# Attention scores issued for two units at a time in the first stage of a transformer layer kernel

## The reference

```python
qkv = (x @ w_qkv).reshape(Bx, Lx, 3, NUM_HEADS, HEAD_DIM)
scores = jnp.einsum('bhqd,bhkd->bhqk', q, k) / np.sqrt(HEAD_DIM)
scores = jnp.where(causal, jnp.finfo(scores.dtype).min, scores)
out = jnp.einsum('bhqk,bhkd->bhqd', softmax(scores), v)
x = layernorm(x + out @ w_out)
# ternary: weights to -1, 0, 1 by |w| > 0.5 * mean|w|; the input over its rms
h = gelu(ternary_linear(x, w_up), approximate=False)
x = layernorm(x + ternary_linear(h, w_down))
```

## Time and profile before

| | us |
|---|---|
| median of 3 runs | 2260.82 (2260.28 to 2261.11) |
| the profiled execution | 2259.11 |
| its span, slowest core | 2257.2 (cores 2249.8 to 2257.2) |
| PE busy | 2135.0 (95%) |
| ACT busy | 1349.5 (60%) |
| DVE busy | 1237.7 (55%) |
| POOL busy | 355.3 (16%) |

### The profile page before, as it was taken

One profiled execution on the slowest core, in us unless ns is written; L12 is line 12 of the kernel. 1 busy time (PEld: TensorE's weight loads), 2 busy tenths in 40 slices (PEclk: granted clock), 3 DMA queues, 4 the chain that ended last, 5 costly groups with the idle time before them and its releaser, 6 DMA issues.

```text
span 2257.2 us, 54506 instructions; the slowest of 8 cores (2249.8 to 2257.2 us)
## 1 busy us (share of the span) xinstructions
PE 2135.0 (95%) x21250; PEld 1313.1 (58%) x21250; DVE 1237.7 (55%) x2100; ACT 1349.5 (60%) x1436; POOL 355.3 (16%) x574
## 2 busy tenths in 40 slices
PE   5999999998899999889999999999999999999998
PEld 2555555555455555466566656656656656566665
DVE  2455555677777533365566555645635545445654
ACT  1589888888788898732444444455465565755111
POOL 3222121222222122101100110110110110101110
PEclk9999999999999999989999999999999999999999
DMA  9135343353545113311000101100101100101100
GB/s 155 34 118 155 114 131 128 111 169 122 155 146 162 42 23 106 125 53 45 32 29 36 50 20 36 41 27 32 39 20 30 47 20 20 47 5 39 38 20 19
DMA packets 77946, 154.70 MB, mean 69 GB/s; under 512 B 27392, under 2 KB 45952, under 8 KB 76672
## 3 DMA queue, kind: packets, MB, share of 16 engines
q1 hardware_dynamic: 70880, 134.44, 17.8%
q0 software_dynamic: 6816, 16.78, 4.7%
HBM read 134.42 MB, written 33.55 MB: 74 GB/s over the span
## 4 chain that ended last, share of the span: by engine, by line
PE 84%; DVE 6%; ACT 5%; issue 4%; DMA 1%; DVEq 0%; POOL 0%; SPq 0%; ACTq 0%; POOLq 0%
PE mm L76 60%; PE sc L76 13%; PE pv L76 11%; ACT pb L76 3%; ACT L76 1%; DVE kt L76 1%; DVE wneg L76 1%; DMA xT<-xt 1%; DVE nrm L76 1%; DVE ast L76 1%; DMA yb<-x 1%; DVE vs L76 0%; DVE qt L76 0%; DVE pb L76 0%; DVE yb L76 0%
## 5 line engine op out<-in xcount | busy, mean ns | idle before, releaser
L76 ACT ACTIVATE pb<-sc,bias 128x1024 bf16<-128x1024 f32 (+3 forms) x1152 | 1160.7, 1042 | 449.8 <-PE sc L76 434.6
L76 PE MATMUL mm<-wdn,hT 128*128 128x512 fp8e4 x2048 | 479.3, 380 | 0.0
L76 PEld LDWEIGHTS pv<-vs,pb 128*128 128x128 bf16 x8448 | 365.5, 98 | 174.6 <-issue 48.0
L76 PE MATMUL pv<-vs,pb 128*128 128x65 bf16 x8448 | 410.1, 194 | 29.0 <-DVE ast L76 16.7
L76 ACT ACTIVATE hT<-mm 128x512 bf16<-128x512 f32 x256 | 152.9, 597 | 343.3 <-PE mm L76 342.7
L76 PEld LDWEIGHTS mm<-wdn,hT 128*128 128x128 bf16 x2048 | 186.6, 98 | 243.7 <-issue 51.7
L76 PE MATMUL mm<-xT,wq 128*128 128x512 bf16 x1024 | 307.9, 391 | 15.5 <-DMA xT<-xt 15.5
L76 PE MATMUL sc<-qt,kt 64*128 64x512 bf16 (+3 forms) x1440 | 270.0, 372 | 3.0 <-ACT pb L76 2.6
L76 PE MATMUL mm<-xnT,wupa 128*128 128x256 bf16 x2048 | 231.5, 274 | 2.3 <-ACT hT L76 1.3
L76 PEld LDWEIGHTS mm<-xnT,wupa 128*128 128x128 fp8e4 x2048 | 198.2, 98 | 28.7 <-issue 4.3
L76 DVE TENSOR_TENSOR hsq<-hT 128x512 f32<-128x512 bf16 x240 | 166.0, 692 | 56.2 <-ACT hT L76 52.1
(11 more groups left out here) (63 smaller groups left out, 1765.6 us busy)
## 6 DMA issues: line engine op xcount, KB each, us to landing
wr<-w_up SPq DMA_DIRECT2D x64, 512.0 KB, 3.6
wr<-w_down SPq DMA_DIRECT2D x64, 512.0 KB, 3.6
yb<-x SPq DMA_DIRECT2D x32, 512.0 KB, 3.2
out<-yb SPq DMA_DIRECT2D x32, 512.0 KB, 2.6
xT<-xt POOLq DMA_DIRECT2D x16, 512.0 KB, 35.9
wq<-w_qkv POOLq DMA_DIRECT2D x24, 256.0 KB, 8.9
att_s<-ast SPq DMA_DIRECT2D x40, 128.0 KB, 2.8
atto<-att_s SPq DMA_DIRECT2D x8, 640.0 KB, 4.2
```

What stands on the lines that cost most here:

```text
L76: ins = ops[op](*args, **kw)
```

## The change

The loop of the first stage takes the units two by two. It issues the scores of both, adds up their widths, works out the rate once, and then pulls, lets the weights go on and drains once for both, with the summed width. In the order on PE that gives: scores of u, scores of u + 1, the pieces of both, pv of u - 2, pv of u - 1.

```diff
-            for unit in units:
-                wide = min(4, 4 - (unit[2] - 4 * unit[1])) / 4.0
-                emit_qk(*unit)
-                left = work.left()
-                rate = left / max(to_do, 1.0)
+            for two_units in zip(units[0::2], units[1::2]):
+                wide = 0.0
+                for unit in two_units:
+                    wide += min(4, 4 - (unit[2] - 4 * unit[1])) / 4.0
+                    emit_qk(*unit)
+                rate = work.left() / max(to_do, 1.0)
                 if p == 0 and c < 5:
                     rate = max(rate, 2 * QKV_NS / (4 * c + 2.5))
                 to_do -= wide
                 work.pull(rate * wide)
                 if p > 0 or c >= 4:
                     side_pull(0.27 * wide)
                 drain(LAG)
```

## The result

| | before | after |
|---|---|---|
| median of 6 runs, us | 2260.97 (2259.44 to 2268.51) | 2309.39 (2305.59 to 2309.9, and one of 2432.63) |
| ratio, 95% interval | | 1.0206 (1.019 to 1.0223) |
| a later set of runs, ratio | | 1.0214 (1.0196 to 1.0232) |

The change makes the kernel 48 us slower; 2314 us were forecast, within 2280 to 2340.

The account below looks back on a forecast made before the run. PE was taken as the bound, ACT close behind. 16 - 6 + 45 + 5 - 4 = +56 us, less 3 for hidden DVE waits, gave 2312 us on the profiled execution, 2314 as median; range 2280 to 2340.

Parts of the forecast that it names:

- The bank stalls: First-stage norm and bound matmuls sharing a pair with their group's end wait 0.66 us for eviction: +45 and +5 us.
- The windows that keep a boundary: Norm and bound matmuls with pv and scores still between get 0.47 us more cover: -4 us.
- the walk over eight pairs: Pair spacings reckoned from PE work and exponential delay, scores 314.63 to 333.31 us: 18.68 becomes 19.06, with stalls 21.04.
- The hand-over: A pair's second scores wait for the previous pair's second exponential, 2.64 us spacing: net +16 us from the sixth chunk.
- the saving: First stage: a pair costs PE 0.21 us less than two units, at most 77 us over 366 pairs.
- ACT needs the same: four exponentials back to back take 4.43 us, 1.11 each: First stage: ACT needs 1.11 us per exponential, as PE needs 1.10 to 1.11 us per unit with one piece.
- +2 us at most, taken as nothing: Between chunks, 0.1 us less cover for DVE's output scaling, some 16 waits; assumed covered by PE's wait at second scores.
- What stays: Pieces, pv matmuls and DVE, POOL and SP instructions keep number and order; no new wait for pb.
- The signs: Profile after: score waits 40 us or more, blk and o64 some 75, spacings 2.2 and 2.64, stage some 975 us.
- The clock: Rival: the granted clock falls often in the first stage, adding some 25 us, 2340 us; chance 0.09.
- The drain rival: From scores to full-height matmuls, -0.21 us a pair wins if second scores seldom wait for ACT: 2230 us; chance 0.07.
- The upper bound: Half of the bank stalls double through DVE's queue, +22 us on top: 2338 us.

Follow-up runs that it names:

- after_again: The changed kernel run once more with no edit, for a profile to read: median 2308.3 us.
- half exponentials: First-stage exponentials over the left half of each head's columns only: changed kernel 2233.45 us, kernel before 2246.51 us.

## Why the prediction was right, and where it was not

**The bank stalls** were right in mechanism, and nearly in size. Along the trace of after_again, from the sixth chunk on, 75 norm and bound matmuls have their group's end in the same pair (74 counted ahead), with 65.1 us of stalls, a median of 0.68 us each and 1.32 us from the last matmul's start; the other 84 wait 7.4 us in all, where 8 were left by the estimate. (A stall is counted here with its 0.16 us of drain.) Over the whole stage the change brought 77 such matmuls into one pair with their group's end, 76 by the prediction. By idle time they waited 11.8 us in 19 places in the kernel before, which the prediction took as nothing, and 54.5 us in 76 places after; with the drain that is 52 us more, against 50 in the sum. The windows that keep a boundary idled 11.6 us before, where the prediction read 16, and 5.6 after. At the end 36 us arrive, and 46 were in the sum (45 + 5 - 4): that each 0.66 arrives in full came out of the walk over eight pairs, and does not hold in the whole stage.

**The hand-over** was right in mechanism. Its net with the saving was near too (+10 in the sum, +12 in the runs), but that was luck: two errors cancel. The step "ACT needs the same: four exponentials back to back take 4.43 us, 1.11 each" failed. They were back to back because PE delivered scores every 1.11 us. ACT's own pace is 1.01 us between starts, as 331.47 and 332.48 show, and rows that I could have read in the kernel before, where two exponentials in the second stage take 2.12 us and one 1.11:

```profile
1501.14 2.12 ACT L76 ACTIVATE pb<-sc,bias 128x1024 bf16<-128x1024 f32 x2 [1.61 <-PE sc L76]
...
1511.91 1.11 ACT L76 ACTIVATE pb<-sc,bias 128x1024 bf16<-128x1024 f32 x1 [1.61 <-PE sc L76]
```

The length of a row is not its share of the engine: 0.11 us of it overlaps with the next. The Trainium skill, "Perfetto Trace Analysis", DVE / Act Engine Instruction, says why: the end that the profiler reports for such an instruction is the acknowledgment of the last write, while the next may start its reads when the execution is over. The rows agree with it.

With 2.12 in place of 2.22 the next second scores start 0.27 + 2.12 + 0.15 = 2.54 us after these, not 2.64. Of 259 pairs of full units in the trace of after_again, from the sixth chunk on, 90 have a spacing between 2.5 and 2.6 us, the commonest by far, and 3 between 2.6 and 2.68. That takes a good part of the hand-over's 87 us away (10 net, after 77 saved); 55.5 were measured.

The other error was the **saving**, 77 us in the sum. 65.5 us of it are there in PE's busy time, and 44 at the end, because DVE's waits come up when the cover shrinks. "+2 us at most, taken as nothing" for the scaling failed in the runs without ACT's wait (11 us), and was passed in the changed kernel as it is (16.7 to 21.1 us), though there the waits at the pv matmuls fell in all, from 27.8 to 24.2 us.

Put right, the walk still does not close. With 65.5 / 366 = 0.18 us saved a pair, exponentials that start 1.01 us apart, and the bank stalls, the same two lines (from the sixth chunk on; PE's work alone before it), over all pairs from the starts of the scores in the trace of the kernel before, come to some 60 to 70 us, an estimate after the fact, where 48 were measured. One reason may be that the single units' times, which the walk takes as PE's own work, hold ACT's 14 us already; no run settles it.

**What stays** stood: the instructions are the same in number, and the second stage takes the same. **The signs** read here held too: score waits of 51.9 us where 40 or more were named, 75 us at blk and o64 as named, and a stage of 969 us where some 975 were; only the longer spacing is 2.54, not 2.64. **The clock** rival has at most some 7 us of the 48; its price of 25 us was not worked out from rows. **The drain rival** (2230 us) is near what half exponentials show, 2233, but it was not right for that: it has the pairs 31 us under single units, and with ACT out of the way they are 13 under. Its condition, that second scores seldom wait for ACT, was wrong in the kernel as it is. The upper bound, 22 on top of 2314, is 2336 and not 2338; nothing rests on it. The rule of the Trainium skill, "TensorEngine Tiling (Array Packing)", Key Properties, that a change of tiling mode drains the engine, agrees with PE's busy time in the runs (65.5 us less for the same matmuls); it says nothing of who waits for what is moved together. The "take off 3" for waits that hide was not separable.

## A kernel that beats both

The kernel before with the norm matmuls one piece later: 2226.99 us, 0.9854 (0.984 to 0.9869) of the kernel before, with all of the reference's work done. It changes two digits of the source.

## What to carry to other kernels

Before putting two producers' steps back to back to save a switch, write down what the second one waits for and what stands behind it in the queue: with two buffers, the second of a pair waits for the consumer's whole previous pair, and every later matmul with it. Moving work together also moves apart-standing pairs of producer and reader together; look for matmuls whose cover was the work that now lies elsewhere, here one-piece windows that lost their 0.67 us. And take an engine's pace from starts in a stretch where its input was waiting, not from the length of rows or from a stretch in which its producer sets the beat.

## What was not expected of the hardware

An exponential over 128 x 1024 is shown with 1.11 us and costs ACT 1.01. The idle time in PE's rows understates a wait by some 0.16 us (0.37 shown, 0.53 lost). And ACT, which by the rows held PE up for 3.3 us, gave the kernel before 14 us when its work was halved.
